# A gated attention and mixture-of-experts block on one core: the written order of the pieces on all five queues set anew

## Chip, core and metric

The kernel runs on one core of a Trainium2 chip. The metric is device microseconds (us) of one execution, and the median over the runs is what is compared. Lower is better.

## What is computed

The reference takes `x` (4 batches of 512 rows of 512 numbers) and a context `ctx` (4 x 512 x 128), and applies two gated additions. In the first, a similarity matrix per batch is built from the context, thresholded at its 153 largest entries per row, made symmetric, and mixed with a layer norm of `x`:

```python
sim = einsum(Q, K) / (sqrt(d) * H)                  # 512 x 512 per batch
mask = sim >= (153rd largest of the row)
A = sigmoid(sim) * mask;  A = (A + A^T) / 2
x = x + tanh(g_xattn) * ((1 - gamma) * layernorm(x) + gamma * A)
```

The second is a feed-forward part with 8 experts, of which each of the 2048 rows takes two, and one shared expert:

```python
t = layernorm(x)
top2 = top_k(t @ router_w, 2);  p = sigmoid(top2 values)
shared = silu(t @ Wg) * (t @ Wu) @ Wd
expert_out = sum over experts e of (silu(p_e t @ gate_e) * (p_e t @ up_e)) @ down_e
x = x + tanh(g_ffn) * (shared + expert_out)
```

## The kernel before, in words

One function, `flamingo_gated_block`, holds five instruction streams, one each for SyncE (`sp`), GpSimd (`pool`), ScalarE (`act`), TensorE (`pe`) and VectorE (`dve`). In each stream small helper functions are defined, and below them stands a list of calls, written out by hand. The list is the order of the work on that engine. An engine runs its list strictly in that order; semaphores inside the helpers (`wait_ge`, `then_inc`) hold a piece back until what it needs is there. So a list can be permuted without adding or removing work, and what changes is who waits for whom.

The work goes through four batches, b = 0 to 3, each of four row tiles, i = 0 to 3:

- **Context and similarity.** `load_ctx(b)` (L333) brings the context; TensorE turns it over (`turn_ctx`, L931), multiplies by the product of the two weight matrices (`turn_q`, L938) and makes the four tiles of similarities (`sim_tile`, L943). ScalarE copies each result out of PSUM (`turned_ctx` L580, `turned_q` L584, `sim_of` L589).
- **Threshold search.** VectorE takes the statistics of a sample of the similarities (`sim_stats`, L1371), GpSimd takes a root (`spread`), and `first_probe` (L1381) makes a first guess. Four rounds follow, k = 0 to 3: VectorE counts some of the tiles (`count`, L1390), ScalarE the others (`sign`, L594), and `move` (L1396 to L1400) shifts the guess. `last_count` (L1409), `best_below` (L1427, L1431), `threshold` (L1436), `check_search` and `mask_sim` (L1463) finish it. ScalarE makes the values that are masked (`value`, L609 and L612) and the layer norm of `x` (`affine`, L623); VectorE takes the row statistics of `x` (`row_stats`, L1350).
- **Mix and second norm.** TensorE turns the masked matrix over (`turn_a`, L953 and L956), VectorE adds it (`add_turned`, L1481), takes statistics (`mixed_stats`, `mixed_spread`), GpSimd takes the root (`root_of_mixed`, L469), `normal_in` (L1501) prepares and ScalarE writes the normed rows (`normal`, L631). TensorE turns them over (`turn_x2`, L963) and ScalarE copies (`turned_x2`, L642).
- **Routing.** `route`, `turned_logits`, `turn_logits`, then on VectorE `pick_experts`, `rank_tokens`, `one_hots`, with `rank_pairs` and `table` on TensorE. After batch 1 a first plan of nine tiles is made (`count_pairs(0)`, `order_columns(0)`, `name_rows(0)`, `read_plan(0)`), after batch 3 the second plan of thirty.
- **Jobs.** There are 55 jobs. Sixteen are of the shared expert (S) and 39 of gathered rows (M): jobs 0 to 7 are S, 8 to 11 M, 12 to 15 S, 16 to 18 M, 19 to 22 S, 23 to 54 M. A job is `up(j)` on TensorE (L1044 for S, L1048 for M), `silu_of(j)` on ScalarE, `gate(j)` on VectorE (L1647, L1642), for M also `turn_h(j)` (L1058), then `down(j)` (L1074) and `y_of(j)` (L692). Results of an S job are added to the output by `shared` (L475), those of an M job by the indirect `scatter` (L508); every scatter waits for the one before it. An M job first needs `gather(t)` (L492) and `turn_rows(t)` (L1026). The S jobs of a batch need its `turn_x2` alone, so they are what TensorE can do while the searches of later batches run.
- **Clock keepers.** `warm(n, count)` (L915) issues products of ones that nothing reads; they go to a bank of `down`.

The SyncE list also decides in which order the loads enter its one queue: contexts, `load_x(b)` (L339), the experts' weights `load_gu(e)` (L345, 1024 KB) and `load_dn(e)` (L349, 512 KB), the shared weights (`load_shared`, L373 to L375) and the stores `store_base`, `store_rows`, `store_payload`.

Three helpers with a wait that matters below. VectorE waits for the share of the count that ScalarE does; TensorE waits for a context to land; and the train of 18 warming products waits for the search of batch 0:

```python
def move(b, k):
    ...
    dve.wait_ge(sign_ready, (COUNTS - 1) * b + k + 1)

def turn_ctx(b):
    pe.wait_ge(ctx_loaded[b], 16)

def warm(n, count):
    if n == 1:
        pe.wait_ge(top8_ready, 2)
```

Of the kernel before, what the change touches and what calls it, by code (L numbers as in the profile page):

```python
# [25 lines left out]
def flamingo_gated_block(nc, x, ctx_in, g_xattn, g_ffn, wq, wk, gamma_raw, router_w, gate_up_w, down_w,  # L26
# [71 lines left out]
    with ExitStack() as stack:  # L98
# [148 lines left out]
        qT_ready = sem("qT_ready")  # L247
# [83 lines left out]
        def _(sp):  # L331
# [100 lines left out]
        def _(pool):  # L432
# [83 lines left out]
            root_of_mixed(0)  # L516
            root_of_mixed(1)
            root_of_rows(1)
            spread(2)
            shared(0)  # L520
            root_of_mixed(2)
            shared(1)
            shared(2)
            root_of_rows(2)
# [3 lines left out]
            spread(3)  # L528
            gather(3)
            shared(3)  # L530
            shared(4)
            gather(4)
            shared(5)
            shared(6)
            gather(5)
            gather(6)
            root_of_mixed(3)
            gather(7)
            root_of_rows(3)
            shared(7)  # L540
            gather(8)
# [5 lines left out]
            root_of_mixed(4)  # L547
            shared(13)
            shared(14)
            shared(15)  # L550
# [3 lines left out]
            gather(10)  # L554
            scatter(6)
            shared(19)
            shared(20)
            shared(21)
# [15 lines left out]
        def _(act):  # L574
# [150 lines left out]
            affine(0)  # L725
            value(0, (2, 3))
            sign(1, 0)
            turned_ctx(3)
            normal(0, 0)
            sign(1, 1)  # L730
            turned_x2(0, 0)
            sim_of(2, 3)
            sign(1, 2)
            normal(0, 1)
            normal(0, 2)
            normal(0, 3)
            turned_x2(0, 1)
            sign(1, 3)
            silu_of(0)
            turned_q(3)  # L740
            silu_of(1)
            turned_x2(0, 2)
            turned_x2(0, 3)
            sim_of(3, 0)
            turned_logits(0)
            read_bad(1)
# [1128 lines left out]
```

## Time and profile before

| what | us |
|---|---|
| median of three runs | 413.25 (413.23 to 413.89) |
| the profiled execution's own time | 412.82 |
| its span, first to last instruction | 411.1 |
| TensorE busy | 381.6 (93%) |
| VectorE busy | 182.1 (44%) |
| ScalarE busy | 187.0 (45%) |
| GpSimd busy | 132.0 (32%) |
| weight loads into TensorE | 219.2 (53%) |

The profile is of one execution. Times in it count from the start of the span. "Idle before" in a row is the time in which the engine stood still ahead of the row, with what ended it. Busy TensorE time is modelled from pipelined instructions, so it says when the engine had work and not how well it was used. The granted clock is given as a share of the full 2.4 GHz.

### The profile page before, as it was taken

Reading aid. Unit: us, or ns where it says so; the run is one execution under the profiler, and the core shown is the slowest. Engines: PE = TensorE matmul, PEld = TensorE weight load, DVE = VectorE, ACT = ScalarE, POOL = GpSimd, SP = SyncE. Lnnn points to the kernel's source line nnn. Section 1 sums busy time; section 2 is a strip of 40 time slices with the busy share of each in tenths; the row PEclk is TensorE's granted clock in tenths of the full one; section 3 lists DMA queues with packets and bytes.
Section 4 is the critical chain, followed back from the end, with each engine's and each line's share of the span. In section 5 each row is a group of like instructions: output and inputs, shape, how many; then the busy total and the mean of one; then the engine's idle time right before and its main releaser. Section 6 shows DMA issues by size and latency. Waiting matters only on the chain.

```text
span 411.1 us, 5817 instructions
## 1 busy us (share of the span) xinstructions
PE 381.6 (93%) x1702; PEld 219.2 (53%) x1702; DVE 182.1 (44%) x746; ACT 187.0 (45%) x397; POOL 132.0 (32%) x124
## 2 busy tenths in 40 slices
PE   8769689889999999999999999999999999999970
PEld 3324478467755787568844444444444444444430
DVE  1899989998998698834510111101110111001000
ACT  4493967484673696262123433323333332333320
POOL 2100111110634323033042345554443554445331
PEclk9968899999999999999999999999999999999996
DMA  7999960093576542385253555545555544555331
GB/s 218 385 387 381 370 217 13 15 241 122 185 128 183 163 66 28 51 225 88 27 103 53 103 103 97 89 84 98 99 103 104 91 82 87 103 105 103 50 48 29
DMA packets 30469, 53.72 MB, mean 131 GB/s; under 512 B 4774, under 2 KB 8102, under 8 KB 30438
## 3 DMA queue, kind: packets, MB, share of 16 engines
q0 software_dynamic: 11040, 24.81, 34.5%
q1 hardware_dynamic: 19110, 28.40, 19.7%
q8 instruction: 15, 0.25, 0.3%
q10 hardware_dynamic: 288, 0.13, 0.1%
q14 instruction: 16, 0.13, 0.1%
HBM read 29.93 MB, written 23.40 MB: 130 GB/s over the span
## 4 chain that ended last, share of the span: by engine, by line
DMA 38%; PE 34%; issue 10%; DVE 7%; ACT 5%; POOL 1%; POOLq 1%; SPq 1%; DVEq 0%; ACTq 0%
DMA out_dram<-y_sb,idx 36%; PE gate_up L1044 14%; PE down L1074 8%; PE gate_up L1048 6%; DMA xs<-in_x_dram 2%; PE front L953 1%; DVE statx L1350 1%; PE front L963 1%; ACT junk L594 1%; PE turned_x L1026 1%; DMA xg<-x_rows,idx 1%; POOL out_dram L475 1%; ACT sim L589 1%; PE front L956 1%; ACT y_sb L692 1%
## 5 line engine op out<-in xcount | busy, mean ns | idle before, releaser
L1048 PE MATMUL gate_up<-w_gu,xT 128*128 x312 | 139.9, 593 | 0.0
L508 POOL DMA_INDIRECT out_dram<-y_sb,idx x39 | 62.1, 1592 | 112.6 <-DMA out_dram<-y_sb,idx 79.5
L1048 PEld LDWEIGHTS gate_up<-w_gu,xT 128*128 128x128 f32 x312 | 56.9, 190 | 60.5 <-issue 60.3
L1642 DVE SCALAR_TENSOR_TENSOR h<-gate_up,p_t,silu 128x256 f32<-128x256 f32 x39 | 18.8, 483 | 136.4 <-ACT silu L665 119.2
L1074 PE MATMUL down<-w_dn,hT 128*128 x156 | 73.7, 596 | 0.5 <-ACT hT L674 0.5
L1044 PE MATMUL gate_up<-xT,w_shgu 128*128 128x128 f32 x512 | 61.5, 281 | 2.2 <-issue 1.9
L692 ACT ACTIVATE y_sb<-down,gates 128x512 f32<-128x512 f32 x55 | 37.7, 687 | 55.1 <-PE down L1074 43.1
L1044 PEld LDWEIGHTS gate_up<-xT,w_shgu 128*128 128x128 f32 x512 | 60.2, 196 | 4.2 <-issue 3.9
L665 ACT ACTIVATE silu<-gate_up,p_t 128x256 f32<-128x256 f32 x39 | 18.5, 474 | 84.4 <-PE gate_up L1048 83.8
L492 POOL DMA_INDIRECT xg<-x_rows,idx x39 | 40.1, 1029 | 44.0 <-DMA x_rows<-payl 15.7
L1074 PEld LDWEIGHTS down<-w_dn,hT 128*128 128x128 f32 x156 | 26.7, 190 | 20.9 <-issue 20.9
L594 ACT ACTIVATE junk<-sim,probe 128x512 int8<-128x512 f32 x44 | 31.2, 711 | 13.8 <-DVE probe L1381 9.9
L683 ACT COPY xT<-turned_x 128x512 f32<-128x512 f32 x39 | 22.8, 585 | 18.4 <-PE turned_x L1026 18.4
L1074 PE MATMUL down<-w_shdn,hT 128*128 128x512 f32 x64 | 30.2, 598 | 0.0
L1026 PEld LDWEIGHTS turned_x<-ident,xg 128*128 128x128 f32 x156 | 19.1, 141 | 18.6 <-issue 18.0
L475 POOL DMA_DIRECT2D out_dram<-y_sb x16 | 15.5, 1009 | 41.1 <-ACT y_sb L692 41.1
L1632 DVE SCALAR_TENSOR_TENSOR p_junk<-xg,oh_e 128x8 f32<-128x8 f32 x39 | 6.2, 163 | 41.0 <-DMA xg<-x_rows,idx 40.8
L1026 PE MATMUL turned_x<-ident,xg 128*128 128x128 f32 x156 | 23.5, 273 | 0.8 <-issue 0.8
L1058 PEld LDWEIGHTS turned_h<-ident,h 128*128 128x128 f32 x78 | 10.7, 141 | 19.5 <-issue 16.6
L674 ACT COPY hT<-turned_h 128x256 f32<-128x256 f32 x39 | 14.3, 366 | 6.0 <-PE turned_h L1058 6.0
L1058 PE MATMUL turned_h<-ident,h 128*128 128x128 f32 x78 | 15.0, 274 | 1.1 <-DVE h L1642 1.1
L1074 PEld LDWEIGHTS down<-w_shdn,hT 128*128 128x128 f32 x64 | 11.1, 190 | 8.6 <-issue 8.6
(181 smaller groups left out, 393.9 us busy)
## 6 DMA issues: line engine op xcount, KB each, us to landing
w_gu<-in_L_ffn_gate_up_w_dram SPq DMA_DIRECT2D x8, 1024.0 KB, 12.0
xs<-in_x_dram SPq DMA_DIRECT2D x4, 1024.0 KB, 7.4
w_dn<-in_L_ffn_down_w_dram SPq DMA_DIRECT2D x8, 512.0 KB, 11.2
out_dram<-xs SPq DMA_DIRECT2D x4, 1024.0 KB, 6.4
x_rows<-x SPq DMA_DIRECT2D x4, 1024.0 KB, 4.8
out_dram<-y_sb POOLq DMA_DIRECT2D x16, 256.0 KB, 4.6
w_gu<-in_ctx_dram SPq DMA_DIRECT2D x4, 256.0 KB, 5.6
xg<-x_rows,idx POOLq DMA_INDIRECT x39, 4.0
```

The costliest lines, as they stand in the source:

```text
L475: G.dma_start(out_v[n // RT][:, n % RT], y_sb[:, j % 2], accum_op=ALU.add).then_inc(shared_out[j % 2], 16)
L492: G.indirect_dma_start(out=xg[:, t % XG, :], out_offset=None, in_=x2_rows[0:2 * N, :] if t < EARLY else x2_rows[:, :], in_offset=bass.Indi ...
L508: G.indirect_dma_start(out=out[0:2 * N, :] if t < EARLY else out[:, :], out_offset=bass.IndirectOffsetOnAxis(ap=idx[:, t:t + 1], axis=0), ...
L594: ins = A.activation(junk[:, i - SHARE[b]], sim[:, b, i], ACT.Sign, scale=-1.0, bias=probe[:, k, i:i + 1], accum_out=sgn[:, k, i:i + 1])
L683: A.copy(xT[:, x_slot(j)], x_b[:, :].rearrange("p (c t) -> p c t", c=DC)).then_inc(xt_done, 1)
L692: A.activation(y_sb[:, j % 2], y_b[j % 2][:, :], ACT.Copy, scale=gates[:, 1:2]).then_inc(y_done, 1)
L1026: mm = TE.transpose(x_b[:, c * P:(c + 1) * P], xg[:, t % XG, c * P:(c + 1) * P], ident[:, :])
L1044: mm = TE.matmul(g_b[j % 2][:, f * P:(f + 1) * P], w_shgu[:, c, f * P:(f + 1) * P], xT[:, x_slot(j), c], start=(c == 0), stop=(c == DC - 1))
L1048: mm = TE.matmul(g_b[j % 2][:, :], xT[:, x_slot(j), c], w_gu[:, bass.ds(experts[n] * (DC * F2) + c * F2, F2)], start=(c == 0), stop=(c == ...
L1058: mm = TE.transpose(h_b[:, c * P:(c + 1) * P], h[:, c * P:(c + 1) * P], ident[:, :])
L1074: mm = TE.matmul(y_b[j % 2][:, :], hT[:, j % 2, c], w, start=(c == 0), stop=(c == IC - 1))
L1642: V.scalar_tensor_tensor(h[:, :], g_b[j % 2][:, I:F2], p_t[:, t % XG:t % XG + 1], silu[:, :], ALU.mult, ALU.mult).then_inc(h_ready, 1)
```

## The change

The lists of calls are permuted on SyncE, GpSimd, ScalarE, TensorE and VectorE. No helper is altered, no call is added or taken away. The repeating middle (jobs 27 to 48, a loop in each list) stays as it is; behind it a few neighbours are swapped. The core of the diff, by engine; a line of only "..." marks what is left out.

```diff
 # SyncE
             load_x(0)
+            load_gu(0)
             load_ctx(2)
+            load_dn(0)
             load_ctx(3)
-            load_gu(0)
-            load_dn(0)
-            load_x(1)
             load_gu(1)
...
             load_dn(3)
+            store_zeros()
+            load_shared()
             load_gu(4)
-            store_zeros()
             load_dn(4)
             load_dn(5)
-            load_shared()
             load_dn(6)
+            load_x(1)
             load_dn(7)
             load_gu(5)
-            load_gu(6)
             store_base(0)
             store_rows(0)
             load_x(2)
+            load_gu(6)
+            store_base(1)
             store_rows(1)
             store_payload(0)
-            store_base(1)
             load_x(3)
             store_payload(1)
             load_gu(7)
+            store_rows(2)
+            store_payload(2)
             store_base(2)
-            store_rows(2)
             store_base(3)
-            store_payload(2)
 # ScalarE
             sim_of(0, 0)
+            sim_of(0, 1)
             turned_ctx(1)
-            sim_of(0, 1)
...
             turned_ctx(2)
+            sign(0, 0)
             turned_q(1)
-            sign(0, 0)
             sign(0, 1)
-            turned_q(2)
             sign(0, 2)
             sim_of(1, 0)
-            sign(0, 3)
-            value(0, (0, 1))
             sim_of(1, 1)
             sim_of(1, 2)
             sim_of(1, 3)
+            turned_ctx(3)
+            sign(0, 3)
+            turned_q(2)
+            value(0, (0, 1))
+            value(0, (2, 3))
+            affine(0)
+            read_bad(0)
             sim_of(2, 0)
             sim_of(2, 1)
-            read_bad(0)
             sim_of(2, 2)
...
+            y_of(2)
+            y_of(3)
+            turned_logits(1)
+            sign(2, 0)
             sim_of(3, 2)
-            y_of(2)
-            turned_logits(1)
 # TensorE
             turn_ctx(2)
             turn_q(1)
-            pe.wait_ge(sim_ready, 4)
-            warm(3, 2)
             pe.wait_ge(ctxT_ready, 3)
             turn_ctx(3)
             sim_tile(1, 0)
+            pe.wait_ge(sim_ready, 4)
+            warm(3, 2)
+            turn_q(2)
             pe.wait_ge(gates_ready, 1)
             sim_tile(1, 1)
             sim_tile(1, 2)
-            turn_q(2)
             sim_tile(1, 3)
+            pe.wait_ge(qT_ready, 3)
+            turn_q(3)
             sim_tile(2, 0)
             sim_tile(2, 1)
...
             check_search(0)
+            sim_tile(2, 2)
+            sim_tile(2, 3)
             pe.wait_ge(sim_ready, 10)
             warm(1, 18)
+            warm(4, 3)
+            sim_tile(3, 0)
             turn_a(0, 0)
...
             rank_pairs(0)
             down(2)
+            down(3)
             pe.wait_ge(at_used, 7)
             turn_x2(1, 0)
...
             route(1)
-            pe.wait_ge(y_done, 2)
-            warm(4, 3)
             turn_logits(1)
             up(4)
             rank_pairs(1)
-            pe.wait_ge(logit_used, 2)
-            count_pairs(0)
...
             up(5)
-            order_columns(0)
-            down(3)
+            pe.wait_ge(logit_used, 2)
+            count_pairs(0)
             pe.wait_ge(table_used, 1)
             table(1)
+            order_columns(0)
+            down(4)
             name_rows(0)
             up(6)
             up(7)
-            down(4)
...
             turn_rows(0)
-            check_search(2)
             down(5)
             turn_rows(1)
             up(8)
+            check_search(2)
             up(9)
             turn_rows(2)
             down(6)
             turn_rows(3)
             turn_h(8)
+            down(7)
             turn_a(2, 0)
 # VectorE
             count(0, 3)
+            sim_stats(1)
             move(0, 3)
             last_count(0)
             best_below(0)
+            first_probe(1)
             threshold(0)
             check_search(0)
             mask_sim(0)
-            sim_stats(1)
-            add_turned(0, 0)
-            mixed_stats(0, 0)
-            add_turned(0, 1)
-            first_probe(1)
-            mixed_stats(0, 1)
-            add_turned(0, 2)
-            mixed_spread(0)
             count(1, 0)
             move(1, 0)
+            count(1, 1)
+            add_turned(0, 0)
+            add_turned(0, 1)
...
-            gate(0)
             last_count(1)
+            gate(0)
             best_below(1)
...
             mixed_spread(2)
             rank_tokens(0)
             normal_in(2)
             weigh_experts(0)
+            first_probe(2)
+            count(2, 0)
             one_hots(0)
-            count(2, 0)
             row_stats(2)
-            move(2, 0)
             pick_experts(1)
             sum_pairs(0)
+            weigh_experts(1)
...
-            weigh_experts(1)
```

On GpSimd `root_of_rows(1)` goes ahead of `root_of_mixed(1)`, `shared(3)` ahead of `gather(0)`, `gather(8)` ahead of `root_of_rows(3)`, and `gather(10)` behind `shared(20)`. From batch 2 on the same kind of permutation goes on in all lists: for example on VectorE `count(3, 0)`, `move(3, 0)` and `count(3, 1)` go between the pieces of batch 2's mix, on TensorE `turn_rows(7)` goes to right behind `route(3)`, and `turn_rows(9)` from behind `up(24)` to ahead of it.

## Rows read from the trace of the kernel before

**Rows 1.** The page: busy tenths of TensorE and its granted clock, 40 slices

```profile
PE   8769689889999999999999999999999999999970
PEclk9968899999999999999999999999999999999996
```

**Rows 2.** By stretch: length, busy of PE, PEld, DVE, ACT, POOL; clock, DMA share, GB/s

```profile
0.00:101.12 101.12, 84.89 (x474) 52.86 (x475) 84.37 (x348) 65.59 (x146) 13.70 (x29) 0.93 0.71 238
80.50:101.12 20.62, 17.15 (x149) 13.10 (x149) 18.89 (x102) 13.81 (x31) 3.29 (x4) 1.00 0.63 180
101.12:390.20 289.08, 288.35 (x1208) 162.89 (x1207) 97.25 (x398) 118.11 (x246) 113.64 (x92) 1.00 0.51 99
21.20:27.80 6.60, 5.68 (x7) 2.04 (x8) 6.32 (x24) 6.60 (x16) 0.00 (x0) 0.50 1.06 388
```

**Rows 3.** Timeline of TensorE, two successive second products of the repeating middle

```profile
272.06 1.88 PE L1074 MATMUL down<-w_dn,hT 128*128 x4
...
277.87 1.88 PE L1074 MATMUL down<-w_dn,hT 128*128 x4
```

**Rows 4.** The chain that ended last: start, length, what; its load and first and last scatters

```profile
3.30 7.72 DMA xs<-in_x_dram
...
230.18 4.89 DMA out_dram<-y_sb,idx
...
397.04 4.77 DMA out_dram<-y_sb,idx
```

**Rows 5.** Timeline of all engines at the end: last output tile and last scatter

```profile
400.33 0.69 ACT L692 ACTIVATE y_sb<-down,gates 128x512 f32<-128x512 f32 x1 [2.16 <-PE down L1074]
402.56 1.55 POOL L508 DMA_INDIRECT out_dram<-y_sb,idx  x1 [3.97 <-DMA out_dram<-y_sb,idx]
```

**Rows 6.** Timeline of SyncE's queue: issues of expert 0's two loads

```profile
4.94 0.74 SPq L345 DMA_DIRECT2D w_gu<-in_L_ffn_gate_up_w_dram  x1
5.73 2.80 SPq L349 DMA_DIRECT2D w_dn<-in_L_ffn_down_w_dram  x1
```

**Rows 7.** The same two loads among the DMA issues: KB, us from issue to landing

```profile
w_gu<-in_L_ffn_gate_up_w_dram SPq DMA_DIRECT2D x1, 1024.0 KB, 9.5
w_dn<-in_L_ffn_down_w_dram SPq DMA_DIRECT2D x1, 512.0 KB, 11.0
```

**Rows 8.** Timeline of TensorE in the first quarter: start, length, what, [idle before <-releaser]

```profile
9.53 1.88 PE L943 MATMUL down<-w_gu 128*128 128x512 f32 x4
11.95 0.63 PE L931 MATMUL turned_x<-ident,w_gu 128*128 128x128 f32 x4 [0.54 <-DMA w_gu<-in_ctx_dram]
...
21.64 3.78 PE L943 MATMUL down<-w_gu 128*128 128x512 f32 x4 [2.97 <-ACT w_gu L584]
...
31.22 5.75 PE L915 MATMUL down<-ones 128*128 128x512 bf16 x18 [2.24 <-DVE top L1431]
...
61.90 3.74 PE L1044 MATMUL gate_up<-xT,w_shgu 128*128 128x128 f32 x32
...
82.16 1.33 PE L963 MATMUL front<-ident,x 128*128 128x128 f32 x8 [1.61 <-ACT x L631]
...
87.60 0.82 PE L915 MATMUL down<-ones 128*128 128x512 bf16 x3
...
101.12 7.39 PE L1044 MATMUL gate_up<-xT,w_shgu 128*128 128x128 f32 x64
108.35 1.88 PE L1074 MATMUL down<-w_shdn,hT 128*128 128x512 f32 x4
```

**Rows 9.** Timeline of VectorE: last counts, statistics of a batch, the masks of batch 2

```profile
25.43 0.74 DVE L1409 TENSOR_SCALAR_CACHE_REDUCE ge_words<-sim,probe 128x512 uint8<-128x512 f32 x1
...
37.06 1.40 DVE L1371 BATCH_NORM_STATS2 stats<-sim 128x6 f32<-128x256 f32 x4
...
57.23 0.73 DVE L1409 TENSOR_SCALAR_CACHE_REDUCE ge_words<-sim,probe 128x512 uint8<-128x512 f32 x1
...
117.54 2.74 DVE L1463 SCALAR_TENSOR_TENSOR sim<-sim,thr,tmp 128x512 f32<-128x512 f32 x4 [0.69 <-ACT tmp L612]
```

More of the change, by code:

```diff
@@ L528, in _ @@
             spread(3)
+            shared(4)
+            shared(5)
             gather(3)
-            shared(3)
-            shared(4)
             gather(4)
-            shared(5)
             shared(6)
+            shared(7)
             gather(5)
@@ L538, in _ @@
             gather(7)
+            gather(8)
             root_of_rows(3)
-            shared(7)
-            gather(8)
             scatter(0)
@@ L557, in _ @@
             shared(20)
+            gather(10)
             shared(21)
@@ L1081, in _ @@
             turn_q(0)
+            warm(2, 2)
             turn_ctx(1)
-            warm(2, 2)
             sim_tile(0, 0)
@@ L1117, in _ @@
             turn_a(0, 3)
-            turn_q(3)
             pe.wait_ge(at_used, 3)
@@ L1196, in _ @@
             turn_a(2, 1)
-            down(7)
+            up(10)
             pe.wait_ge(at_used, 9)
@@ L1201, in _ @@
             turn_a(2, 3)
-            up(10)
             up(11)
+            turn_h(9)
+            down(8)
+            down(9)
             pe.wait_ge(at_used, 11)
             turn_x2(2, 0)
+            turn_rows(4)
+            turn_h(10)
             pe.wait_ge(at_used, 12)
             turn_x2(2, 1)
-            turn_h(9)
-            down(8)
-            turn_h(10)
+            up(12)
+            turn_h(11)
             pe.wait_ge(x2t_done, 9)
@@ L1214, in _ @@
             turn_x2(2, 3)
-            down(9)
+            down(10)
             route(2)
-            turn_h(11)
-            turn_rows(4)
+            down(11)
             turn_logits(2)
-            up(12)
+            up(13)
             rank_pairs(2)
-            up(13)
-            down(10)
-            down(11)
             up(14)
+            down(12)
             pe.wait_ge(rank_used, 3)
@@ L1242, in _ @@
             turn_a(3, 2)
-            down(14)
+            turn_h(16)
             pe.wait_ge(at_used, 14)
@@ L1250, in _ @@
             turn_x2(3, 0)
+            down(16)
             pe.wait_ge(at_used, 16)
             turn_x2(3, 1)
-            down(16)
+            up(19)
+            turn_h(17)
             pe.wait_ge(x2t_done, 13)
@@ L1257, in _ @@
             turn_x2(3, 3)
-            up(19)
-            turn_h(17)
+            down(17)
             route(3)
-            down(17)
+            turn_rows(7)
             turn_h(18)
@@ L1265, in _ @@
             rank_pairs(3)
-            down(18)
             up(21)
@@ L1269, in _ @@
             count_pairs(1)
-            up(22)
+            down(18)
             order_columns(1)
@@ L1273, in _ @@
             table(3)
-            turn_rows(7)
+            down(19)
             name_rows(1)
-            down(19)
+            up(22)
+            down(20)
             turn_rows(8)
-            down(20)
             up(23)
+            turn_rows(9)
             up(24)
-            turn_rows(9)
-            down(21)
             up(25)
@@ L1285, in _ @@
             turn_rows(10)
+            down(21)
             down(22)
@@ L1708, in _ @@
             add_turned(1, 0)
-            gate(2)
-            first_probe(2)
             add_turned(1, 1)
@@ L1714, in _ @@
             add_turned(1, 2)
+            gate(2)
+            mixed_stats(1, 2)
             add_turned(1, 3)
-            mixed_stats(1, 2)
             mixed_stats(1, 3)
@@ L1770, in _ @@
             mixed_spread(3)
-            normal_in(3)
+            gate(10)
             weight_of(4)
-            row_stats(3)
-            gate(10)
-            row_affine(3)
             weight_of(5)
             weight_of(6)
+            normal_in(3)
+            row_stats(3)
+            count(3, 2)
+            move(3, 2)
+            row_affine(3)
             gate(11)
+            count(3, 3)
             weight_of(7)
-            count(3, 0)
-            move(3, 0)
-            count(3, 1)
+            move(3, 3)
+            last_count(3)
+            gate(12)
             pick_experts(2)
-            move(3, 1)
-            count(3, 2)
+            weigh_experts(2)
             rank_tokens(2)
-            move(3, 2)
             one_hots(2)
-            gate(12)
-            count(3, 3)
-            move(3, 3)
             gate(13)
-            last_count(3)
+            gate(14)
+            add_table(2)
             best_below(3)
-            add_table(2)
             threshold(3)
-            gate(14)
             check_search(3)
@@ L1802, in _ @@
             add_turned(3, 0)
+            gate(16)
             mixed_stats(3, 0)
-            gate(16)
-            weight_of(8)
             add_turned(3, 1)
```

237 lines of the change are left out of this document (117 added, 120 removed).

## Prediction, made before the changed kernel was run

> **What bounds the kernel now.** I read first the page's two lines by slices. TensorE is short of work only in the first ten slices, about 103 us; behind them it is full until the end, at full clock [rows 1]. The table of busy time by stretch puts numbers on it: up to 101.12 us TensorE is busy 84.89 of 101.12, so it stands still for 16.2; from there to 390.2 it stands still for 289.08 - 288.35 = 0.7 [rows 2]. The amount of work on TensorE is the same before and after, warming products included. So the change can gain at most those 16 us and what the lower clock costs in the first quarter, and anything it gains must come from having more of TensorE's work done by about 101 us.
>
> Second, the chain of waits says who owns the end. From 230.18 it is one unbroken run of indirect scatters, each waiting for the one before [rows 4]. TensorE's own period in that part is 277.87 - 272.06 = 5.81 us per job [rows 3]; the scatters go at (397.04 - 230.18) / 30 intervals = 5.56. They start with a backlog, because three second products come close together, and work it off at 0.25 a job. At the end the last output tile is done at 400.33 + 0.69 = 401.02 and its scatter starts at 402.56 [rows 5]. The two limits are thus 1.5 us apart, and both begin at the same point: the second product of job 23. The order behind that point is nearly unchanged, so an earlier job 23 moves both, and the end follows one for one. The reader need only follow how early TensorE gets there.
>
> Third, the first quarter. VectorE is busy 84.37 of its 101.12 us, of which the first 11 are mostly the wait for `x` [rows 2, 4]. From there on VectorE's list is the clock by which the first 80 us go, and TensorE waits for it.
>
> **The change, part by part.**
>
> *SyncE.* Expert 0's two loads go ahead of the contexts of batches 2 and 3, and `x` of batch 1 goes far back. `x` of batch 0 keeps its place; it lands 3.30 + 7.72 = 11.02, and I leave that. Context 2 had landed by 11.95, where TensorE began on it [rows 8]. The four loads together were in by 5.73 + 11.0 = 16.7, the gate/up load alone by 4.94 + 9.5 = 14.4 [rows 6, 7]. If the queue serves roughly in order, context 2 now lands near 14.4 and context 3 near 16.7. Bounds: not before 11.9; not later than issue (about 8, behind the same 2.80 us issue) plus 11.0 to 12, so 20. I take 14.4 and 16.7, the rows of the very bytes that stand ahead. The page "DMA: Bandwidth & Descriptors" of the Trainium skill, section "Two DMAs through the same engine are not ordered", says that nothing orders transfers across the 16 engines; by it context 3 could land anywhere in these bounds, and only a landing past 19 would cost. The shared weights go forward and hide; `x` of batch 1 lands by about 43 and is read at 49.
>
> *First search, 11 to 37 us.* `sim_stats(1)` goes ahead of the last move of batch 0. It takes 2.0 us on VectorE (1.40 for the four tiles [rows 9], and some 0.6 for the small pieces behind them), and `first_probe(1)` another 0.3. So the masks of batch 0 end 2.3 later. That is work brought forward, not added. It needs the four tiles of batch 1 in SBUF at 24.9: TensorE has context 3 at 16.7, the turned product at 19.5, then one tile, two warming products, `turn_q(2)` and three tiles. At full clock one tile takes 1.88 / 2 = 0.94, back to back 0.86, so the last is there at 24.2 and its copy at 24.9. At the lower clock a tile takes 3.78 / 2 = 1.9 [rows 8].
>
> *The warming train.* `warm(1, 18)`, `warm(4, 3)` and a tile now stand together ahead of `turn_a(0, 0)`. The train can start when ScalarE has copied `sim_of(2, 1)`, near 35.3, since `value`, `affine` and the rest now come before it. 18 products take 18 x 0.21 = 3.8 at full clock (the three at 87.60: 0.64 until the next piece), 5.75 in the trace where half of them ran slow [rows 8]. With 0.6 and 0.9 behind it, `turn_a(0, 0)` starts at 40.6, against masks done at 39.3. VectorE fills part of that with `count(1, 0)` and stands still for 1.3. I follow the rest of the list with the same durations: `last_count(1)` starts at 57.3, where it stood at 57.23, since `gate(0)` now stands behind it and a wait of VectorE for ScalarE's share of the count falls away. TensorE starts `up(2)` at 61.7 for 61.90 [rows 8, 9]. Up to here the change is worth nothing.
>
> *62 to 101 us, where it pays.* TensorE waited 1.61 at 82.16 for the normed rows of batch 1 [rows 8]. `first_probe(2)` is moved behind the statistics, so the rows come some 0.6 earlier; and `down(3)`, 1.72 between starts, now stands ahead of that wait and fills it. So `turn_x2(1, 0)` starts at about the old 82.1 with one product more done. `warm(4, 3)`, 0.64, has gone from this stretch to the train. With shorter waits between the four turned tiles (about 0.5) `up(4)` starts 1.1 earlier. `down(4)` is moved ahead of `name_rows(0)`, where TensorE waited for VectorE's tables, so `up(6)` starts at 100.1 for 101.12, with `down(4)` done as well, which used to stand at 108.35 [rows 8]. Lead: 1.0 + 1.7 = 2.7 us. It cannot be more than the 20.62 - 17.15 = 3.5 us of idle in 80.5 to 101.12 plus the 0.6 of warming [rows 2]. I take off 0.5 for the handoffs between engines that I did not time one by one: 2.2.
>
> *Behind 101 us.* TensorE is full, so a lead stays if nothing runs dry. `payload(1)` used to be made late on VectorE and held the first gather; `weigh_experts(1)` is now ten us earlier, so gathers start about four earlier and cover the lead. The tightest handoffs: `check_search(2)` is moved behind `up(8)`, two us behind the flags it reads; `turn_a(2, 0)` goes behind `down(7)` at 121.3, and the masks of batch 2, 117.54 + 2.74 before, should end at 120.3 [rows 9]. One us of slack. The second plan's gathers have some 9 us of products ahead of `turn_rows(9)` for 5.5 of latency. These edits I cost at nothing; if that cover goes, TensorE waits for exactly the shortfall.
>
> *Sum.* Span 411.1 - 2.2 = 408.9, the execution's own time 412.82 - 2.2 = 410.6. The median stands 0.43 above the profiled run: 411.0.
>
> **The rivals.**
>
> *A lower clock for batch 1's tiles.* In the trace TensorE stood still for 2.97 us ahead of 21.64, and from 21.20 to 27.80 the granted clock is 0.50, that is 1.2 GHz [rows 2, 8]. After the change it waits longer for context 2, some 3 us instead of 0.54. If the lower level then covers the tiles of batch 1, they come 1.5 us late, `sim_stats(1)` holds all of VectorE, and of the gain 0.7 is left: 412.5. The section "HAM oscillation — how this bites in real kernels" of the Trainium skill's page "TensorE: Matmul & The Clock Gate" describes just this, a wait for a transfer after which matmuls run cold. Against it: in the trace that stretch ran slow already and the new order has more work in it.
>
> *Slower: the train runs slow as well.* The 21 warming products now all stand ahead of `turn_a(0, 0)`. If the lower level holds over them, they take twice as long, up to 21 x 0.21 = 4.4 more, together with 1.5 from above and less the gain: about +2.3, 415.5. It decides from the point where train and tiles cost more than 2.2 together. For it: the trace has exactly this level at the train's start, 5.75 for 18 products [rows 8]. Against: five products of tiles now run right ahead of it.
>
> *No change: the lead runs into VectorE.* The search of batch 2 is hardly earlier than before; if the masks come two us later than I work out, TensorE waits at `turn_a(2, 0)` and the lead is gone: 413.2.
>
> *The order does not do what it says* is no rival of weight: lists are in order, and waits only add.
>
> **How the numbers follow.** Forecast, a lead of about 2.2 kept: 0.5. Larger lead, up to 3.7 (409.6): 0.06. Lower clock for the tiles: 0.18, half of it counted as faster. Lead lost to VectorE: 0.11. Slower by the train or a late context: 0.15. About 0.2%, 0.8 us, is what a measurement of this kernel can tell from no change. Faster 0.5 + 0.06 + 0.09 = 0.65; same 0.09 + 0.11 = 0.20; slower 0.15. The range 409.6 to 413.9 holds the larger lead and the lost one, and leaves out the slow train.
>
> **What would show it.** Right: `turn_ctx(2)` near 14.5, masks of batch 0 ending near 39.3, `last_count(1)` near 57.3, no idle of 1.6 ahead of `turn_x2(1, 0)`, `up(6)` near 100.1 with `down(4)` before it, the scatter after job 23 near 228, and the end of the span near 408.9. Wrong: a clock of 0.50 between 19 and 28 with VectorE idle ahead of `sim_stats(1)`; a train above 5 us; TensorE idle after 110; or scatters whose chain no longer starts with job 23.

## The result and the profile after

The changed kernel takes **416.27 us** in the median of 20 runs (412.63 to 417.57), the kernel before 413.18 beside it (20 runs): ratio 1.0066, interval 1.0048 to 1.0083 (a ratio is taken over the runs, not from the two medians). The change costs some 3 us where 2.2 were forecast as a gain, and the time lies above the range. The profiled execution took 413.98 us with a span of 412.2, so it is one of the changed kernel's quicker ones; part of the loss has to be looked for in other executions.

The page's two lines by slices, TensorE and its granted clock, answer to [rows 1]:

```profile
PE   8578789989999989999999999999999999999960
PEclk9889899999999999999999999999999999999995
```

The table by stretch (columns as in [rows 2]); the last three stretches are those with a lower clock:

```profile
0.00:101.12 101.12, 83.78 (x473) 53.04 (x474) 83.57 (x346) 64.72 (x142) 14.67 (x30) 0.95 0.77 252
80.50:101.12 20.62, 18.71 (x149) 13.30 (x147) 19.36 (x113) 15.09 (x34) 4.71 (x5) 1.00 0.88 242
101.12:390.20 289.08, 287.42 (x1208) 162.12 (x1206) 98.09 (x400) 120.07 (x250) 111.79 (x91) 1.00 0.50 95
14.40:17.90 3.50, 3.19 (x10) 1.55 (x8) 2.74 (x17) 1.55 (x4) 1.36 (x2) 0.51 1.06 377
28.10:31.50 3.40, 3.40 (x6) 0.86 (x4) 3.33 (x13) 3.40 (x7) 0.00 (x0) 0.50 1.09 375
48.60:52.00 3.40, 2.84 (x13) 2.87 (x14) 3.33 (x11) 3.28 (x8) 0.07 (x1) 0.50 0.65 246
```

The repair from 80.5 to 101.12 is there: busy 18.71 of 20.62, for 17.15 before. But the mean busy time up to 101.12 is not larger, TensorE stands still for 1.7 us behind 101.12 where it was 0.7, and the lower clock has moved: not on batch 1's tiles as in [rows 2], but on batch 2's context and batch 1's `turn_q`, on batch 2's tiles, and on the first product of the shared expert, `up(0)`. The timeline of TensorE shows these places, columns as in [rows 8]:

```profile
14.18 0.85 PE L931 MATMUL turned_x<-ident,w_gu 128*128 128x128 f32 x4 [2.76 <-DMA w_gu<-in_ctx_dram]
...
18.98 1.12 PE L943 MATMUL gate_up<-w_gu 128*128 128x512 f32 x2 [1.39 <-ACT w_gu L584]
...
27.02 1.13 PE L938 MATMUL turned_h<-w_gu,y_sb 128*128 128x512 f32 x2 [3.05 <-ACT w_gu L584]
27.98 3.50 PE L943 MATMUL down<-w_gu 128*128 128x512 f32 x4
...
35.22 4.52 PE L915 MATMUL down<-ones 128*128 128x512 bf16 x20 [1.73 <-ACT sim L589]
...
40.43 0.60 PE L953 MATMUL front<-ident,sim 128*128 128x128 f32 x4
...
47.81 0.63 PE L963 MATMUL front<-ident,x 128*128 128x128 f32 x4 [2.02 <-ACT x L631]
49.16 5.15 PE L1044 MATMUL gate_up<-xT,w_shgu 128*128 128x128 f32 x32 [0.72 <-issue]
...
62.92 3.75 PE L1044 MATMUL gate_up<-xT,w_shgu 128*128 128x128 f32 x32
...
83.42 1.23 PE L963 MATMUL front<-ident,x 128*128 128x128 f32 x8
...
99.69 1.98 PE L1074 MATMUL down<-w_shdn,hT 128*128 128x512 f32 x4 [0.17 <-DVE hT L1645]
...
101.88 7.39 PE L1044 MATMUL gate_up<-xT,w_shgu 128*128 128x128 f32 x64
...
148.41 0.33 PE L979 MATMUL front<-ident,tmp 128*128 128x128 f32 x1 [1.35 <-ACT tmp L650]
...
227.24 1.88 PE L1074 MATMUL down<-w_dn,hT 128*128 x4
```

Read it as a balance against [rows 8]. `up(2)` starts at 62.92 for 61.90: 1.02 lost. `up(6)` starts at 101.88 for 101.12, but with `down(4)`, 1.72, done: 0.96 in hand, so 1.98 was won in between (0.64 of it is `warm(4, 3)`, which now runs ahead of `up(2)`). The second product of job 23, to which both limits of the end are tied, is at 227.24 for 227.30: the 0.96 is gone again. From `up(6)` to there the old kernel took 126.18 and the new 125.36, but with 1.72 less to do it should have been 124.46.

VectorE in the same execution:

```profile
36.24 2.74 DVE L1461 SCALAR_TENSOR_TENSOR sim<-sim,thr,tmp 128x512 f32<-128x512 f32 x4 [0.38 <-DVE sel L1434]
...
57.53 0.16 DVE L1396 SCALAR_TENSOR_TENSOR u<-sgn,stride 128x3 f32<-128x3 f32 x1 [0.93 <-ACT junk L594]
...
57.92 0.75 DVE L1407 TENSOR_SCALAR_CACHE_REDUCE ge_words<-sim,probe 128x512 uint8<-128x512 f32 x1
...
68.67 1.42 DVE L1461 SCALAR_TENSOR_TENSOR sim<-sim,thr,tmp 128x512 f32<-128x512 f32 x2 [1.48 <-issue]
```

The masks of batch 0 end at 36.24 + 2.74 = 38.98, 1.45 before TensorE turns them at 40.43: the train of warming products, not VectorE, now sets that start. The wait of 0.93 ahead of 57.53 is for ScalarE's last share of the count; the old kernel had it too, with 1.23 ahead of 56.49. The 1.48 ahead of the masks of batch 1 was not there before.

The loss behind 101 us shows on GpSimd and ScalarE, in these rows of the two timelines:

```profile
139.61 1.66 POOL L508 DMA_INDIRECT out_dram<-y_sb,idx  x1 [0.20 <-issue]
...
147.51 0.69 ACT L692 ACTIVATE y_sb<-down,gates 128x512 f32<-128x512 f32 x1 [3.29 <-DMA out_dram<-y_sb,idx]
148.10 0.26 ACT L650 COPY tmp<-front 128x128 f32<-128x128 f32 x1
```

`y_of(10)` writes the buffer that the first scatter reads, so it waits 3.29 us for that scatter to land; the turned logits of batch 2 stand behind it on ScalarE, and TensorE waits 1.35 for them at 148.41. It is ScalarE's own list that brings this about: in the old one `turned_logits(2)` stood ahead of `y_of(9)` and `y_of(10)`, and waited for no scatter, as ScalarE's timeline of the old kernel shows:

```profile
139.89 0.27 ACT L650 COPY tmp<-front 128x128 f32<-128x128 f32 x1 [1.76 <-PE front L973]
```

The end answers to [rows 4, 5], first the chain of waits, then the timeline:

```profile
230.13 4.85 DMA out_dram<-y_sb,idx
...
398.31 4.70 DMA out_dram<-y_sb,idx
```

```profile
400.46 0.69 ACT L692 ACTIVATE y_sb<-down,gates 128x512 f32<-128x512 f32 x1 [2.16 <-PE down L1074]
...
403.76 1.55 POOL L508 DMA_INDIRECT out_dram<-y_sb,idx  x1 [3.91 <-DMA out_dram<-y_sb,idx]
```

The scatters start at the old time (230.13 for 230.18) and their last one is 1.20 later: (403.76 - 230.13) / 31 = 5.60 per scatter for (402.56 - 230.18) / 31 = 5.56. The loop of the middle is the same in both kernels and only a few neighbours behind it are swapped, so this looks like variation of a chain of transfers from one execution to the next (over the profiles with whole scatters the interval is 5.56 to 5.69). It is all of the 1.1 us by which the two profiled spans differ. The typical loss must be shown in another way.

### The profile page after: what moved, and what is told of

It reads as the page before. It is cut to its first block, busy times and chain, and to the rows that moved or that the text cites. A ratio compares the mean times of both kernels' runs of the same rounds, so it can differ in the third digit from the quotient of the medians.

```text
span 412.2 us, 5814 instructions
## 1 busy us (share of the span) xinstructions
PE 379.5 (92%) x1701; PEld 218.7 (53%) x1702; DVE 182.1 (44%) x746; ACT 188.2 (46%) x397; POOL 131.1 (32%) x124
## 4 chain that ended last, share of the span: by engine, by line
DMA 36%; PE 16%; issue 8%; ACT 2%; POOL 1%; POOLq 1%; ACTq 0%
DMA out_dram<-y_sb,idx 36%; PE gate_up L1044 6%; PE down L1074 4%; PE gate_up L1048 3%; ACT y_sb L692 2%; PE turned_x L1026 1%; POOL xg L492 1%; POOLq L98 0%; PE front L953 0%; PE front L963 0%; POOL out_dram L475 0%; PE front L973 0%; PE front L992 0%; PE turned_h L1058 0%; PE front L979 0%
## 5 line engine op out<-in xcount | busy, mean ns | idle before, releaser
L631 ACT ACTIVATE x<-xs,x2add,pow2out 128x512 f32<-128x512 f32 x16 | 12.3, 807 | 10.2 <-DVE x2add L1499 10.2
```

## The experiments

Ratios are to the kernel before, run on the same chip in the same rounds. "Job 23" is the start of its second product. The two kernels themselves came first, for their spread and to see other executions.

> The changed kernel once more, timed beside the old one on one chip, for a second profile of it. Its first profile has a span of 412.2, 1.1 above the old one, while its runs stand some 3 us above. Theory A (the first quarter differs from execution to execution, by where the lower clock falls): this profile may show a stretch at clock 0.50 over the tiles of batch 1 or the warming train, and up(6) later than 101.9 by 1 to 3 us. Theory B (the loss lies behind 101 us, in the scatter chain or in new waits): up(6) again near 101.9, and the ratio to the old kernel near 1.006 with the difference made behind it.

> The old kernel once more, unchanged, for a second profile and for the scatter of its times. Both theories: ratio 1.000 within 0.2%. Theory A: up(6) starts within 0.5 us of 101.1. Theory B: the mean distance of two scatters between job 23 and the end is again near 5.56 us.

Measured: the new 416.91, ratio 1.0056 (1.0024 to 1.0087); the old against itself 0.999 (0.9966 to 1.0014). The new profile repeats the first one nearly to the row: `up(0)` 5.14 us long, `up(2)` at 62.71, job 23 at 226.87, TensorE idle for 1.24 near 148. The old has `up(0)` at full clock, 3.81, `up(2)` at 60.81 and job 23 at 226.23. So the old order too has executions with and without that cost.

**Halves.** New lists up to `turn_rows(0)` with the old ones behind, and the other way round.

> The new lists up to turn_rows(0) (about 109 us) with the whole new SyncE list, the old lists behind. Theory A: all of the loss is in here, ratio about 1.006 or 414 to 417 us. Theory B: TensorE reaches up(6) with down(4) done, 1 us ahead of the old kernel, and the old remainder keeps it: about 412, ratio 0.998.

> The old lists and the old SyncE list up to turn_rows(0), the new lists behind. Theory A: same as the old kernel, ratio 1.000. Theory B: the loss is in here, ratio 1.006 to 1.010 (415.5 to 417), since the lead of 1 us is missing as well.

Measured: 429.94, ratio 1.0369 (1.0333 to 1.0406), and 421.8, ratio 1.0174 (1.0141 to 1.0206). Both are worse than either kernel. In the first TensorE stands still for 9.54 us ahead of a `turn_x2` at 192.18; in the second for a gather, in this row of its timeline:

```profile
113.90 1.12 PE L1026 MATMUL turned_x<-ident,xg 128*128 128x128 f32 x4 [4.23 <-DMA xg<-x_rows,idx]
```

Each half of an order is made for the arrival times of the other, so the split does not divide the effect. It did give one reading: the new front in the first of them had `up(0)` 6.74 us long and `up(2)` at 65.30, later than in the two profiles of the new kernel.

**The flags of batch 1 earlier**, for the wait of 1.48:

```diff
 # TensorE
             route(0)
+            check_search(1)
             turn_logits(0)
             up(2)
-            check_search(1)
 # ScalarE
+            read_bad(1)
             affine(1)
             value(1, (0, 1))
-            read_bad(1)
```

> The new kernel with one piece put back on two engines: check_search(1) on TensorE ahead of turn_logits(0) and up(2), read_bad(1) on ScalarE ahead of affine(1). In the new profile VectorE stands still 1.48 us at 68.67, until the flags of batch 1's search, made behind up(2), are copied and read. Theory A2 (the front's new waits of VectorE are the loss): the 1.48 goes, up(6) starts 1.0 to 1.5 us earlier (near 100.6), and the ratio to the old kernel falls from 1.006 to about 1.003. Theory B (scatter chain): the ratio stays at 1.006.

Measured: 417.88, ratio 1.0073 (1.0044 to 1.0102), no gain. The wait is gone, but from `up(2)` to `up(6)` it takes 38.67 instead of 38.96: the 1.48 was worth 0.3 to TensorE. The profile shows another case of the front. TensorE's timeline, then its clock in a table by stretch:

```profile
18.78 2.07 PE L943 MATMUL gate_up<-w_gu 128*128 128x512 f32 x2 [1.45 <-ACT w_gu L584]
...
37.84 6.42 PE L915 MATMUL down<-ones 128*128 128x512 bf16 x21 [2.61 <-DVE top L1429]
...
44.95 0.27 PE L953 MATMUL front<-ident,sim 128*128 128x128 f32 x1
```

```profile
14.70:25.00 10.30, 8.71 (x15) 3.29 (x14) 8.76 (x39) 6.03 (x15) 1.01 (x1) 0.50 1.06 385
```

Here the lower level stays on from 14.7 to 25.0, `turn_q(2)` and the first two tiles of batch 1 are made at it (the other two take 1.90 from 24.91, full clock), VectorE waits 1.18 + 0.43 + 0.43 for the tiles in `sim_stats(1)`, and the train runs slow as well: `turn_a(0, 0)` at 44.95 for 40.43. `up(0)` then has full clock (3.81), behind the same two waits of 2.02 and 0.72 us as in the new kernel.

**SyncE's order**: contexts 2 and 3 ahead of expert 0's loads.

```diff
             load_x(0)
-            load_gu(0)
             load_ctx(2)
-            load_dn(0)
             load_ctx(3)
+            load_gu(0)
+            load_dn(0)
```

> The new kernel with contexts 2 and 3 loaded ahead of expert 0's weights again, as in the old one. Theory A (a longer wait of TensorE for context 2 brings the lower clock near batch 1's tiles in some executions, 1 to 3 us): no idle of 2.8 us ahead of turn_ctx(2), ratio down to 1.002 to 1.004 and a smaller spread of the times. Theory B: unchanged, 1.006.

Measured: 418.36, ratio 1.0091 (1.0055 to 1.0127). The contexts are turned at 11.59 and 12.92 instead of 14.18 and 16.53, and nothing is won: the tile behind them starts at 18.38 for 18.98, now after a wait of 4.80 for ScalarE's copy. Its profile shows `up(0)` at the lower level for most of its length, on TensorE and then on VectorE:

```profile
50.30 6.59 PE L1044 MATMUL gate_up<-xT,w_shgu 128*128 128x128 f32 x32 [0.72 <-issue]
```

```profile
60.11 0.16 DVE L1396 SCALAR_TENSOR_TENSOR u<-sgn,stride 128x3 f32<-128x3 f32 x1 [2.44 <-ACT junk L594]
```

`turned_x2(0, 1)` stands on ScalarE ahead of `sign(1, 3)`, and it waits for a product that stands behind `up(0)` on TensorE. So a slow `up(0)` reaches VectorE: it waits 2.44 instead of the 0.93 of the new kernel's first profile.

**A lighter scatter**, in both kernels: only rows 0 to 63 of each tile are scattered, so the expert part of rows 64 to 127 is missing from the output.

> The old kernel with each indirect scatter writing 64 of its 128 rows (the other rows of the expert part are left out of the output). Takes load off the scatter chain. Theory B (the chain owns the end): the chain's period falls below TensorE's 5.81, the end is TensorE's, and the time falls by 1 to 2 us. Theory A: as said, for the old kernel both limits are 1.5 us apart, so also about 1.5 us less.

> The new kernel with each indirect scatter writing 64 of its 128 rows (the other rows of the expert part are left out). Theory B: the new order only suffers in the chain, so with it light it is level with the old one of the same kind (ratio of the two 0.998 to 1.001). Theory A: TensorE itself arrives later in the typical execution, so the two stay 2 to 3 us apart as before.

Measured: old 411.92, ratio 0.9934 (0.9907 to 0.9962); new 413.34, ratio 0.996 (0.9929 to 0.9991). GpSimd's timeline in the old one, two neighbours near the chain's start and two later:

```profile
228.95 1.48 POOL L508 DMA_INDIRECT out_dram<-y_sb,idx  x1 [3.14 <-DVE p_junk L1632]
...
233.50 1.46 POOL L508 DMA_INDIRECT out_dram<-y_sb,idx  x1 [1.76 <-ACT y_sb L692]
...
273.70 1.44 POOL L508 DMA_INDIRECT out_dram<-y_sb,idx  x1 [3.06 <-ACT y_sb L692]
...
279.51 1.44 POOL L508 DMA_INDIRECT out_dram<-y_sb,idx  x1 [3.06 <-ACT y_sb L692]
```

The backlog is worked off at 4.55 each, then the interval is TensorE's own 5.81 and each scatter waits for ScalarE. So with full scatters the chain does own the end in both kernels: by 414.25 - 411.92 = 2.3 us in the old one. In the new one, which was not run whole on this chip, the ratios give some 4: (1.0066 - 0.996) x 414 = 4.4, or 4.0 with the 1.0056 of the repetition. The new one's runs differ more: the two at a mean granted clock of 0.989 took 409.51 and 410.44 us, the three at 0.974 took 412.94, 414.69 and 415.35, the seven between 0.980 and 0.985 took 410.98 to 414.22, and the old one's nine all lie between 410.62 and 413.00 at 0.978 to 0.982. So the same list can be the faster or the slower of the two, and the lower its clock the longer it tends to take.

**No stillness ahead of the tiles and `up(0)`.** That can be tried: warming products in the places where TensorE stands still anyway (four places in the new list, three in the old).

```diff
 # the new list (the old: 13 behind sim_tile(1, 3), 8 ahead of warm(1, 18), 8 ahead of up(0))
             sim_tile(0, 3)
             pe.wait_ge(ctxT_ready, 2)
+            pe.wait_ge(sim_ready, 4)
+            warm(5, 10)
             turn_ctx(2)
...
             turn_ctx(3)
+            warm(6, 5)
             sim_tile(1, 0)
...
             sim_tile(1, 3)
+            warm(7, 13)
             pe.wait_ge(qT_ready, 3)
...
             turn_a(0, 3)
+            warm(8, 9)
             pe.wait_ge(at_used, 3)
             turn_x2(0, 0)
```

> The new kernel with four more groups of warming products (10, 5, 13 and 9) where TensorE stood still: ahead of turn_ctx(2), of sim_tile(1, 0), of turn_q(3) and of turn_x2(0, 0). Five profiles of the new front so far show two cases: up(2) near 62.8 (twice) and near 65.3 to 66.1 (thrice), with the lower clock over batch 1's tiles or over all of up(0) in the second. Theory A (the clock decides which case): no stretch at 0.50 between 12 and 55 us, up(2) at 61 to 62, down(23) near 226, a median 2 to 4 us below the new kernel, ratio to the old one 0.996 to 1.000. Theory C (the order's own waits, whatever the clock): the ratio stays at 1.005 or above.

> The old kernel with warming products at its three idle places (13, 8 and 8). Theory A: up(0) takes 3.6 instead of up to 5.4 and up(2) starts near 60.6, as in its own better executions; median 0.5 to 1 us below the old kernel, ratio 0.998. Theory C: no change, 1.000.

Measured: new **414.0, ratio 0.9996 (0.9973 to 1.0019)**; old 414.95, ratio 1.0014 (0.999 to 1.0039). Work was added and the new list lost its whole deficit; in the old list the same brings nothing that the times show (its profile has `up(6)` at 99.21 for 101.12, but job 23 at 226.36, within the 226.23 to 227.30 of the old kernel's two). Table by stretch, then timeline, of the filled new kernel:

```profile
14.00:50.00 36.00, 31.20 (x119) 14.37 (x121) 31.88 (x114) 25.94 (x59) 3.75 (x4) 1.00 0.94 343
```

```profile
46.61 2.12 PE L915 MATMUL down<-ones 128*128 128x512 bf16 x9
48.79 0.63 PE L963 MATMUL front<-ident,x 128*128 128x128 f32 x4
50.14 3.81 PE L1044 MATMUL gate_up<-xT,w_shgu 128*128 128x128 f32 x32 [0.72 <-issue]
```

Granted clock 1.00 (2.4 GHz) from 14 to 50 us, `up(0)` 3.81, job 23 at 225.55. Of the 1.69 by which job 23 is ahead of the new kernel's first profile, only 0.36 is there at `up(6)` (101.52 for 101.88). The other 1.33 comes behind it, where the first scatter, issued at 139.23 for 139.61, lets `y_of(10)` go after 6.64 us instead of 147.51 - 139.61 = 7.90; TensorE then waits under 0.2 near 147. ScalarE's timeline:

```profile
145.87 0.69 ACT L692 ACTIVATE y_sb<-down,gates 128x512 f32<-128x512 f32 x1 [2.02 <-DMA out_dram<-y_sb,idx]
```

Over all profiles of the new order with whole scatters this time is 7.8 to 8.1 in seven and 6.4 to 7.1 in five, and the five all have fills (of the seven, the kernel with the last fill and a swap). Whether the fills bring that about, no run shows.

**Two waits on ScalarE.** First `sign(1, 3)` ahead of `turned_x2(0, 1)`, then `turned_logits(2)` ahead of `y_of(10)`; each swap is two lines.

> The new kernel with sign(1, 3) on ScalarE ahead of turned_x2(0, 1). In the new order VectorE waits 0.93 to 2.5 us for that sign, because the copy ahead of it waits for a product that TensorE does behind up(0). Theory C (order's own waits): VectorE's wait near 58 to 60 goes, up(2) 1 to 2 us earlier, ratio 1.002. Theory A: only the longer of the two waits belongs to the clock; with the coupling cut up(0) may run slow without harm, and the ratio falls to 1.003.

> The new kernel with turned_logits(2) on ScalarE ahead of y_of(10). In the new profile y_of(10) waits 3.29 us for the first scatter to land, and TensorE stands 1.35 us ahead of turn_logits(2). Theory B2 (the loss behind 101 us is this wait): TensorE's idle near 148 goes, down(23) starts 1.0 to 1.3 earlier relative to up(6), ratio 1.003. Theory A alone: 1.006 unchanged, since the chain starts no earlier.

Measured: 418.42, ratio 1.0099 (1.0068 to 1.013), and 416.63, ratio 1.006 (1.0037 to 1.0083). Both profiles have `up(0)` slow (6.71 and 6.75). In the first the wait for ScalarE's count is gone and stands again a few rows later on VectorE, for a result of the same slow product:

```profile
62.84 0.42 DVE L1645 TENSOR_TENSOR hT<-gate_up,silu 128x256 f32<-128x256 f32 x1 [2.12 <-ACT silu L668]
```

In the second TensorE no longer waits near 148, and from `up(6)` to job 23 it takes 227.99 - 103.48 = 124.51 for 125.36: 0.85 saved, though the median does not show it.

**Which fill.** The one ahead of `turn_x2(0, 0)` alone, and the three earlier ones alone.

> The new kernel with nine warming products ahead of turn_x2(0,0) alone. If up(0) at the lower clock is the price: up(0) takes under 4.2 us instead of 5.15 to 6.7, up(2) starts near 62.6, no wait over 1.2 us of VectorE near 60, ratio to before 0.998 to 1.002. If the price is paid earlier, at batch 1's tiles and in the train: turn_a(0,0) starts as late as before, up(2) at 63.5 or later, ratio 1.004 or more.

> The new kernel with the three fills before 28 us alone. If batch 1's tiles are the price: no lower clock before 40 us, up(2) near 62.6 and ratio about 1.000. If up(0) is the price: the lower clock still falls on up(0) (5.2 to 6.7 us), up(2) at 63.5 to 64.5, ratio 1.003 to 1.006.

Measured: 415.43, ratio 1.0019 (0.9993 to 1.0046), and 414.89, ratio 0.999 (0.9953 to 1.0027). Each half of the fills takes away most of the deficit or all of it, and the times do not tell them apart. TensorE's timelines differ at `up(0)`, the first kernel and then the second:

```profile
49.65 3.81 PE L1044 MATMUL gate_up<-xT,w_shgu 128*128 128x128 f32 x32 [0.72 <-issue]
```

```profile
49.25 5.44 PE L1044 MATMUL gate_up<-xT,w_shgu 128*128 128x128 f32 x32 [0.72 <-issue]
```

So the last fill keeps `up(0)` at full clock, and the early ones do not. But with `up(0)` slow in its profile the second kernel is level with the old one, against what was expected (1.003 to 1.006): a slow `up(0)` by itself is not the 3 us.

**Repairs together.** All fills with `turned_logits(2)` ahead of `y_of(10)`, twice; all fills with the half scatter (rows 64 to 127 missing again); and the last fill with the swap.

> The new kernel with all four fills and the turned logits of batch 2 ahead of y_of(10). If both repairs add up: up(6) near 101.5 and down(23) 0.8 earlier than the 227.5 of the filled kernel, 226.7; span shorter by up to 0.8, ratio 0.998. If the wait at 148 was already gone with the fills: no change from 0.9996.

> All four fills, and only rows 0 to 63 of each tile scattered, so that the expert part of rows 64 to 127 is missing from the output. If the front's fault was the clock alone, the light chain shows TensorE's own lead: 411.0 to 411.9 against 411.92 of the old lists and 413.34 of the new with the same half scatter, ratio to before 0.992 to 0.994. If something else behind 101 us is lost: 412.5 or more.

> The filled kernel with the turned logits of batch 2 ahead of y_of(10), a second time. If it is a gain: ratio 0.9965 to 0.9985 again. If the first time was chance: 0.999 to 1.001, as the filled kernel's 0.9996.

> The turned logits of batch 2 ahead of y_of(10) and only the nine warming products ahead of turn_x2(0,0). If up(0) at the lower clock and the wait at 148 are the two prices: as r17, ratio 0.998 to 1.000. If the early stretches matter by themselves: 1.002 or more, as r13's 1.0019.

| kernel | us | ratio, interval |
|---|---|---|
| fills and swap | 413.42 | 0.9987, 0.9962 to 1.0012 |
| the same again | 414.23 | 1.0012, 0.9991 to 1.0034 |
| last fill and swap | 414.73 | 1.0003, 0.9973 to 1.0034 |
| fills, half scatter (4 runs) | 410.54 | 0.9909, 0.9875 to 0.9943 |

The first ratio did not repeat, and both intervals hold 1: repaired, the new order is level with the old, and no version here with whole scatters is shown to beat the old one. With the light scatter it has 0.9909 for the old order's 0.9934, that is 1.0 us, but the intervals overlap, the chips differ and there are four runs. The profiles say more: in the three with all four fills and whole scatters job 23 is at 223.9 to 225.6, for 227.30 and 226.23 in the old kernel's two, so TensorE has a lead of some 1.8 us there; the scatters' mean interval is 5.62 to 5.64 for 5.56 and 5.61, and 31 of them take most of it back. In the last-fill kernel the profiled execution was the early case again, the lower clock from 14.6 to 24.8, `turn_a(0, 0)` at 44.51 and a span of 415.9; that is what the three early fills are for, and in the five profiles that have them it does not occur.

**Laid side by side**, all profiles of the new front obey one sum. From `turn_a(0, 0)` to `up(2)`, by the length of `up(0)`:

| `up(0)` | profiles | us to `up(2)` |
|---|---|---|
| 3.81 | seven (flags early; all with the last fill) | 21.13 to 21.14 |
| 5.14 to 5.44 | four (the new kernel twice, half scatter, early fills) | 22.47 to 22.77 |
| 6.59 to 6.75 | four (front half, contexts first, both swaps) | 23.98 to 24.08 |

The start of `turn_a(0, 0)` is 39.4 to 41.6 in twelve of the fifteen, and 43.0 to 45.0 in three; in two of these `turn_q(2)` and the first two tiles of batch 1 ran at the lower clock. Without the last fill `up(0)` is slow in eight of nine profiles, with it in none of six. The forecast's own way, 61.7 - 40.6 = 21.1, is the first line of the table.

## Why the prediction was wrong

**What bounds the kernel.** Right. The half scatter shows the chain owning the end by 2.3 us in the old kernel, a little more than the 1.5 of [rows 5], and both limits hang on job 23. That a lead goes through "one for one" holds for its start only: a chain whose mean interval varies from 5.56 to 5.69 between profiles moves the end by up to 31 x 0.13 = 4 us either way.

**SyncE.** Right: context 2 turned at 14.18 (14.4 foreseen), context 3 at 16.53 (16.7). In the runs it did not matter.

**First search.** Right for the profiled execution: masks end 38.98 for 39.3, tiles by 24.

**The train.** Right: it starts at 35.22 for 35.3, `turn_a(0, 0)` at 40.43 for 40.6, and TensorE's lateness against the masks was foreseen at 1.3. Old: masks end at 37.15, and `turn_a(0, 0)` starts at 37.20. New: TensorE is late by 1.45. Fewer products in the train might give that back; it wasn't tried.

**"Up to here the change is worth nothing" is the step that failed**, and with it the sum's other zero, behind 101 us (below). `up(2)` was to start at 61.7. It starts at 62.71 and 62.92 in the two profiles of the new kernel and at 64.5 to 66.1 in six variants without fills, most of them edited elsewhere; in four profiles of the old front at 60.6 to 61.9. I priced `up(0)` at full clock. The lower level falls on it, in most profiles, when TensorE has stood still for 2.02 and 0.72 us just ahead (eight of nine profiles, and none of six with the first of these waits filled), and it costs up to 6.75 - 3.81 = 2.9 us, plus VectorE's longer wait. In three profiles the lateness comes earlier instead, at `turn_a(0, 0)`: 43.0 to 45.0. With the stillness ahead of `up(0)` filled, `up(2)` starts at 60.6 to 62.7 in five of six profiles. The old kernel's timeline had the warning, in a row that I had not chosen:

```profile
47.85 5.44 PE L1044 MATMUL gate_up<-xT,w_shgu 128*128 128x128 f32 x32 [1.91 <-issue]
```

A product of the same shape takes 3.74 at 61.90 [rows 8]. The wait for ScalarE's share of the count that was to fall away is still there as well, 0.93 for 1.23, and `last_count(1)` starts at 57.92 for 57.3.

**62 to 101 us.** Right. `turn_x2(1, 0)` has no idle before it; from `up(2)` to `up(6)` it takes 38.96 for 39.22, with 1.72 more done: 1.98 won. The steps gave 2.5 for this stretch (2.7 less the 0.2 foreseen at `up(2)`), and 2.0 with the 0.5 for handoffs taken off.

**Behind 101 us** "these edits I cost at nothing" was the second miss. The places I named (`check_search(2)`, `turn_a(2, 0)`, `turn_rows(9)`) held. The loss was at one I did not look at: the logits of batch 2 behind `y_of(10)`, which waits for the first scatter. ScalarE's new list puts them there; the old one had them ahead of `y_of(9)`. Moving them back ahead of `y_of(10)` saves 0.85.

**The sum, again.** For TensorE at job 23, new less old: up to 62 us, with the mean of the four profiles of the old front (61.2), 62.8 - 61.2 = +1.6 in the new kernel's own two and 65.3 - 61.2 = +4.1 in the mean of the six variants, where nothing was foreseen; 62 to 101 us -1.98; behind, +0.9. That makes +0.5 to +3.0, and the medians differ by 3.1. It is an estimate: these profiles are single executions that also differ in when their first loads land, and the new kernel's own two, at 413.98 and 414.84 us, are quicker than its medians. That its typical execution looks like the six variants is an inference.

**The rivals.** The two on the clock were the right mechanism, weighed too low (0.33 together) and with the wrong place: not the train for all cases but whatever stands where the engine has just been still, most often `up(0)`. The page "TensorE: Matmul & The Clock Gate" of the Trainium skill, section "HAM oscillation — how this bites in real kernels", has products run cold behind a wait for a transfer; here it also happened behind waits for ScalarE's copies (3.05 us ahead of 27.02, and 0.50 from 28.1). The sum of the slow rival does not come out of its terms: 4.4 + 1.5 - 2.2 is 3.7 and not 2.3, so at its full price it would have been 416.9 and not 415.5. "The lead runs into VectorE" did not come up.

What stays open: how often each case comes, since a run without a profile shows only its mean clock; which of the places in the front carries how much of the 3 us, since either half of the fills removes most of it; why the first scatter lands later in the profiles without fills; and how much of the 3 us is chain variation that the lists influence.

## What to carry to other kernels

An order set from the durations of one trace has that trace's clock built in. Before judging a permutation, list where the engine stands still just ahead of long products and price these at both clock levels, here 3.81 and 6.75 for one product. If the gain hangs on it, put idle-time products there: in the old kernel they changed nothing that could be measured, in the new one they came with a gain of (1.0066 - 0.9996) x 413 = 2.9 us. And look up who owns the end: a lead of TensorE's was hidden here behind a chain of transfers 0.25 a job faster than it, with a backlog.

## What the runs showed of the hardware

- The granted clock fell to 0.50 after TensorE had stood still for 2.76 us (from 14.4) and for 3.05 (from 28.1), and after 2.02 still, 0.63 of work and 0.72 still (from 48.6). The same two waits ahead of `up(0)` left it at 1.00 in the variant with the flags earlier. On which piece it lands changes from execution to execution: the new kernel had it from 14.4 to 17.9, and a variant with edits near 60 us alone had it from 14.7 to 25.0.
- A halved indirect scatter takes 4.55 us in a chain where the whole one takes 5.6. Half of the rows is worth 1.05, so by these two sizes most of its time is not that of its rows.
- Flags that TensorE makes right before they are read hold VectorE ahead of the masks of batch 1 for 1.14 to 1.83 us, in fourteen profiles of the new front; in the variant with the flags earlier it waits 0.18 there, for something else.
- In kernels with the early fills the time outside the span is often larger: 2.3 to 2.7 us instead of 1.7 in 9 of the 12 runs of the second fills-and-swap kernel. Nothing in the profile says why; it takes back part of what the fills win inside the span.
